# Masks of the attention scores: added in the third to sixth turn of the key products, two pieces of the array a turn, instead of ahead of all products

## What is computed

```python
def local_attention(q, k, v):        # WINDOW = 32, QK_SCALE = 8
    bk2, bv2 = (look(bk), look(bv))  # keys and values of the window before and of this one: 64
    mask = (it < jb) | (it > jb + w) | (jb == -1)
    sim = jnp.einsum('bhwie,bhwje->bhwij', bq, bk2) * QK_SCALE
    sim = jnp.where(mask, -jnp.finfo(sim.dtype).max, sim)
    attn = jax.nn.softmax(sim, -1)
    out = jnp.einsum('bhwij,bhwje->bhwie', attn, bv2)
...
for i in range(DEPTH):               # DEPTH = 6
    x = attn_layer(shift_tokens(x), Wqkv[i], q_scale[i], k_scale[i], Wo[i]) + x
    x = ffn_layer(shift_tokens(x), ln_g[i], ln_b[i], W1[i], b1[i], W2[i], b2[i]) + x
return xn_input + attention_branch + x
```

## Time and profile before

| | us |
|---|---|
| time, median of 3 runs | 1501.54 (1500.04 to 1501.63) |
| profiled execution: span from the first to the last instruction | 1500.0 |
| TensorE (PE) busy | 1464.2 (98%) |
| TensorE weight loads (PEld) busy | 1280.8 (85%) |
| VectorE (DVE) busy | 1310.1 (87%) |
| ScalarE (ACT) busy | 1267.7 (85%) |
| GpSimd (POOL) busy | 1248.7 (83%) |
| masks on TensorE | 768 of 387 ns |
| products of queries and keys on TensorE | 12288 records, 225 ns each by the mean |

### The profile page before, as it was taken

One profiled execution on the slowest core, in us unless ns is written; L12 is line 12 of the kernel. 1 busy time (PEld: TensorE's weight loads), 2 busy tenths in 40 slices (PEclk: granted clock), 3 DMA queues, 4 the chain that ended last, 5 costly groups with the idle time before them and its releaser, 6 DMA issues.

```text
span 1500.0 us, 66306 instructions
## 1 busy us (share of the span) xinstructions
PE 1464.2 (98%) x26320; PEld 1280.8 (85%) x26320; DVE 1310.1 (87%) x2365; ACT 1267.7 (85%) x2551; POOL 1248.7 (83%) x1213
## 2 busy tenths in 40 slices
PE   6799999999999999999999999999999999999997
PEld 5578888888888888888888888888888888888886
DVE  6799998889889898888898898889898988998974
ACT  4578888889888888888898888888888888888886
POOL 5489988888888888888888888888888888888781
PEclk9899999999999999999999999999999999999999
DMA  6012212111212111121211121211112121112111
GB/s 185 22 46 60 59 46 57 43 49 42 59 49 79 52 47 43 54 63 52 70 41 50 43 70 49 69 45 50 47 40 55 52 54 38 49 35 52 38 49 39
DMA packets 96184, 80.28 MB, mean 54 GB/s; under 512 B 66282, under 2 KB 79598, under 8 KB 95854
## 3 DMA queue, kind: packets, MB, share of 16 engines
q1 hardware_dynamic: 94990, 75.34, 18.8%
q10 hardware_dynamic: 864, 0.26, 0.1%
HBM read 17.91 MB, written 1.05 MB: 13 GB/s over the span
## 4 chain that ended last, share of the span: by engine, by line
PE 93%; issue 2%; DVE 2%; POOL 1%; ACT 1%; DMA 0%; ACTq 0%; DVEq 0%; POOLq 0%
PE bank L1065 74%; PE bank L1179 11%; PE bank L1217 6%; PE bank L1251 1%; PE bank L1149 1%; DMA rot<-in_b_v 0%; POOL rot L459 0%; DVE parts L891 0%; DVE newton L910 0%; DVE s L937 0%; DVE n L901 0%; DVE am L825 0%; POOL w_lo L446 0%; ACTq L550 0%; ACT rot L576 0%
## 5 line engine op out<-in xcount | busy, mean ns | idle before, releaser
L459 POOL TENSOR_TENSOR rot<-parts 128x512 f32<-128x512 f32 x384 | 493.3, 1285 | 120.4 <-DVE parts L891 120.3
L891 DVE TENSOR_TENSOR parts<-bank,rtab 128x1024 f32<-128x1024 f32 x384 | 459.8, 1208 | 0.4 <-POOL rot L459 0.3
L470 POOL TENSOR_TENSOR rot<-rot,rnorm 128x512 f32<-128x512 f32 x384 | 391.1, 1046 | 10.0 <-DVE rnorm L917 10.0
L901 DVE TENSOR_REDUCE n<-sq 128x8 f32<-128x512 f32 x384 | 257.7, 671 | 33.0 <-ACT sq L627 33.0
L689 ACT ACTIVATE pz<-bank 64x512 f32<-64x512 f32 x384 | 226.1, 589 | 61.4 <-PE bank L1217 59.1
L1065 PE MATMUL bank<-w_hi,x_hi 128*128 128x512 f32 x576 | 263.8, 458 | 4.6 <-DVE parts L891 3.6
L476 POOL TENSOR_TENSOR es<-es,r 128x512 f32<-128x512 f32 x192 | 202.6, 1055 | 75.2 <-DVE r L943 75.2
L627 ACT ACTIVATE sq<-bank 128x512 f32<-128x512 f32 x384 | 230.4, 601 | 28.0 <-DVE n L901 22.0
L1065 PE MATMUL bank<-w_hi,x_lo 128*128 128x512 f32 x576 | 229.5, 398 | 0.0
L1065 PE MATMUL bank<-w_lo,x_hi 128*128 128x512 f32 x576 | 229.1, 398 | 0.0
L1179 PE MATMUL bank<-ident,rot 128*128 128x128 f32 x1536 | 203.1, 275 | 5.0 <-POOL rot L470 2.4
(11 more groups left out here) (86 smaller groups left out, 2660.4 us busy)
## 6 DMA issues: line engine op xcount, KB each, us to landing
vb<-v SPq DMA_DIRECT2D x96, 384.0 KB, 3.8
w_new<-in_Wqkv SPq DMA_DIRECT2D x36, 256.0 KB, 4.2
vb<-v SPq DMA_DIRECT2D x48, 128.0 KB, 3.4
w_o<-in_Wo SPq DMA_DIRECT2D x12, 256.0 KB
xin<-x_tok SPq DMA_DIRECT2D x48, 64.0 KB, 2.1
xs<-x_tok SPq DMA_DIRECT2D x48, 64.0 KB, 2.0
xin<-x_tok SPq DMA_DIRECT2D x48, 56.0 KB, 2.7
xs<-x_tok SPq DMA_DIRECT2D x48, 56.0 KB, 2.0
```

The lines of the kernel that those rows point to most:

```text
L459: g.tensor_tensor(rot[:, i * CH:(i + 1) * CH].rearrange(halves, z=2, c=HD), parts[:, b:b + CH].rearrange(halves, z=2, c=HD), parts[:, b + ...
L470: g.tensor_tensor(c, c, over(r, CHH, DH), ALU.mult).then_inc(s_sc[i], 1)
L891: d.tensor_tensor(parts[:, b:b + 2 * CH].rearrange("p (w h c) -> p w h c", w=2, c=DH), heads(bank[QK_BANK[i]][:, :]).unsqueeze(1).to_broad ...
L901: d.tensor_reduce(n2[:, T * 2 * HEADS + m * CHH:T * 2 * HEADS + (m + 1) * CHH], heads(sq[:, b:b + CH]), op=ALU.add, axis=AX.X).then_inc(s_ ...
```

## The change

The function `score_heads` goes; `score` issues one product and `add_mask` one mask, both for one of the eight pieces (`quadrants`, with the order odd, hh, b). `scores` now runs over ten turns of eight places. A piece gets its mask in turn 2 + k // 2 (counted from 0), that is, pieces 0 and 1 in turn 2, pieces 2 and 3 in turn 3, 4 and 5 in turn 4, 6 and 7 in turn 5. It is left out of the turn after its mask and then goes on with its products. The first product of a piece, not the mask, has the flag that starts an accumulation, and the mask is added to what the piece's bank holds by then (it overwrites the columns that have no product yet; later products accumulate on them). The order of the eight places in a turn is now odd, hh, b, where the products had odd, b, hh. The numbers of masks and products, their operands, the waits ahead of the block and the semaphore at its end stay as they were.

```diff
-            def score_heads(n, T, halves):
-                for half in halves:
-                    for s in range(2):
-                        c = half * 128 + s * 64
-                        for odd in range(2):
-                            pair = 2 * half + odd
-                            for b in range(2):
-                                w = 4 * T + 1 - b + 2 * s
-                                for hh in range(2):
-                                    r, o = 64 * hh, 64 * odd + 32 * (hh ^ b)
-                                    last = mm(bank[S_BANK[T][b]][o:o + WIN, c:c + 64],
-                                              qt3[r:r + DH, pair, WIN * w:WIN * w + WIN],
-                                              kt3[r:r + DH, pair, WIN * w:WIN * w + 64],
-                                              start=False, stop=half == PAIRS // 2 - 1)
-                return last
+            quadrants = [(odd, hh, b) for odd in range(2) for hh in range(2) for b in range(2)]
+
+            def score(n, T, k, i):
+
+                odd, hh, b = quadrants[k]
+                half, s = i // 2, i % 2
+                c, pair, w = half * 128 + s * 64, 2 * half + odd, 4 * T + 1 - b + 2 * s
+                r, o = 64 * hh, 64 * odd + 32 * (hh ^ b)
+                return mm(bank[S_BANK[T][b]][o:o + WIN, c:c + 64],
+                          qt3[r:r + DH, pair, WIN * w:WIN * w + WIN],
+                          kt3[r:r + DH, pair, WIN * w:WIN * w + 64],
+                          start=i == 0, stop=i == PAIRS - 1)
+
+            def add_mask(T, k):
+
+                odd, hh, b = quadrants[k]
+                first = 128 * int(T == 0 and b == 1)
+                r, o = 64 * hh, 64 * odd + 32 * (hh ^ b)
+                mm(bank[S_BANK[T][b]][o:o + WIN, :], identh[r:r + DH, r:r + WIN],
+                   mask[r:r + DH, first:first + 128].unsqueeze(1).to_broadcast([DH, PAIRS // 2, 128]),
+                   start=False, stop=False)
...
                 for i in range(4 * T, 4 * T + 4):
                     pe.wait_ge(s_qte[i], done(n))
-                for odd in range(2):
-                    for hh in range(2):
-                        for b in range(2):
-                            first = 128 * int(T == 0 and b == 1)
-                            r, o = 64 * hh, 64 * odd + 32 * (hh ^ b)
-                            mm(bank[S_BANK[T][b]][o:o + WIN, :], identh[r:r + DH, r:r + WIN],
-                               mask[r:r + DH, first:first + 128].unsqueeze(1).to_broadcast([DH, PAIRS // 2, 128]),
-                               stop=False)
-                score_heads(n, T, range(PAIRS // 2)).then_inc(s_s[T], 1)
+                for turn in range(PAIRS + 2):
+                    for k in range(len(quadrants)):
+                        masked = 2 + k // 2
+                        if turn < masked:
+                            last = score(n, T, k, turn)
+                        elif turn == masked:
+                            add_mask(T, k)
+                        elif turn > masked + 1:
+                            last = score(n, T, k, turn - 2)
+                last.then_inc(s_s[T], 1)
```

## The result

The changed kernel takes 1505.56 us (median of 9 runs, 1504.61 to 1507.16) against 1500.97 us for the kernel before (9 runs beside it). The ratio is 1.0027, with a 95% interval of 1.0018 to 1.0037: slower by 4.6 us, where 10.4 us faster were forecast. The span of the profiled execution went from 1500.0 to 1504.7 us.

What follows compares the result with a forecast made beforehand. TensorE's queue was taken as the bound. Per block, 0.23 us of wait removed less 0.117 for mask places gave 0.113; over 92 blocks 10.4 us, so 1491.1 us from a median of 1501.54, range 1480 to 1512.

Steps and rivals of the forecast that it cites:

- What bounds the kernel: Whole kernel: a queue of TensorE work, busy 98% of the span; edits to it change the span almost one for one.
- The removed wait: Front of each score block: products no longer wait for the masks, gaining 0.23 us a block.
- The price of a place: Eight masks placed among a block's products: 117 ns together, the middle between 78 and 156 ns.
- The piece in time: Turns three to six: a masked piece is free about when its next product is due, after 0.22 to 0.25 us.
- I cost this at nothing, and the cover is other pieces' products: Turns three to six: the 0.23 us mask runs hidden under products on other pieces, at no cost.
- one hold: Rival, chance 0.15 for one or two: a mask oldest in flight holds products behind it; one +0.058 us a block, 1507.
- the extreme: Rival, chance 0.07: shorter products on free pieces cannot start until they would end behind the mask; +0.69 us a block, 1565.
- the order of rows: Rival, chance 0.05: neighbouring products on the same 64 rows wait, 10 ns for each of 32 pairs; 1520 us.

Runs made afterwards that it cites:

- the floor: Masks of the scores left out of the kernel before, products in its old order: 1.413 us a block, span 1479.7 us.
- the halves: Complete kernel with another order than the change: four masks, twelve products on the other four pieces, four masks, the rest; 1.706 us a block.

## Why the prediction was wrong

**What bounds the kernel** was right: TensorE's own row of work sets the time, and 50 ns in each of 96 blocks came out as 4.7 us of span.

**The removed wait** was near: the floor is 1.413 us instead of the 1.388 that follows from subtracting the masks' time. 0.025 us a block were booked as gain that the products had already had.

**The price of a place** was right for masks in turns: 0.124 us for eight against the 0.117 taken, though that was chosen as the middle of two rows 78 ns apart and not derived. What the step missed is that in front a place costs 3.6 ns, since there the instructions stand ready.

**The piece in time** failed in its working. It took some 30 ns for a pass of 64 fp32 columns, from 512 columns of float32r; a record of an fp32 product holds its piece for 0.056 us. So the sentence that every piece stands idle for more than half of the time is wrong: a product takes 0.11 of the 0.156 us in which its piece is asked once. It cost nothing in the change itself, as the masks of 256 columns show; that it is why leaving pieces out for longer makes no room is likely, but not shown.

**"I cost this at nothing, and the cover is other pieces' products"** is the step that failed and turned the sign: after the wait in front was gone, the sum had no term for the masks' length, and that costs 0.128 us a block among products. The piece is indeed free when it is asked for. It is the cover that fails: once a mask is the oldest in flight, no further products arrive, on any piece, until 31 ns behind its end. The sum, as measured: 1.413 + 0.124 + 0.128 = 1.665 us; as predicted, 1.502. Without the last term it would be 1.537, 0.078 us a block faster than before. The mechanism was named as a rival, with a chance of 0.15, at +0.058 us a block and 1507 us for one hold; it measured +0.050 and 1505.6. That these lie so close is partly luck. The rival took one hold of 0.171 us against a gain of 0.113; it was two stops of together 0.128 against a gain of 0.078. Its count of the stretch with the masks was off too: turns three to six hold 18 products and eight masks, not 24 and eight, so 468 ns and not 585. The evidence that was read for it, records in flight that the pieces don't explain, was the right evidence, though the limit was seen at some 33 and not at the 22 of the mean. It was given little weight; nothing in the trace before had a long record among short ones.

**The other rivals:** the extreme is refuted by the halves (products 0.01 us behind the masks), the order of rows by 1.413 against 1.415 us. The prediction took from the Trainium skill (TensorE: Matmul & The Clock Gate, Part 3, "What overlaps and what doesn't") that matmuls keep program order in their ends as well; the records of the change do not: a product's, from 0.331 to 0.569 us, lies inside that of a mask, from 0.267 to 0.640, with the caution that ends are modelled. What does look ordered is the leaving, as a limit on arrivals. The other sentence that it took from the same section of the Trainium skill, that a weight load overlaps running matmuls only where the row groups differ, does not hold here either: in the change the second product's load starts at 0.005 us, while the first product, on the same 64 rows, has its record until 0.240.

## What to carry to other kernels

A long matmul among short ones can cost more than its streaming on its own piece: in these runs it kept its place in flight until it ended, and nothing new arrived once it was the oldest. Try long ones in few groups near the start of a block, where instructions already stand ready (two groups of four took 1.581 us here, four spread pairs 1.665 to 1.679), rather than spread them, and time it; and before spreading, price a place among the others by a version with the same instructions, but short. To see which part of an operation costs, vary its length at several points: 64, 256, 448 and 512 columns told place, piece and flight apart where a single shorter version would not have.

## What the runs showed of the hardware that was not expected

- After a stop, new weight loads of the small products resume 30 to 32 ns after the end of the record that seems to be the oldest in flight, for records of 0.240, 0.347, 0.372 and 0.387 us, though the ends of records are modelled. The load that resumes is the 33rd or so behind that record in the count of records.
- Masks of up to 256 columns (records of up to 0.267 us) cause no stop among these products; with 448 and 512 columns they cost 0.078 and 0.128 us a block.
- A record of an fp32 product with 64 columns holds its piece for 0.056 us, almost twice what the spacing of float32r products suggests (512 columns in 0.23 us, so 64 in 0.03).
- The start of the program differs by up to 3 us between profiled executions of two kernels whose blocks are equal (iteration 11 begins at 345.87 or 348.69 us), while the steady iterations of both take 29.63 to 29.66 us.
